# Graph layer with a mixture of experts on one core: the second norm and the router's scores inside the last edge group, edge steps numbered through all groups, token lists in bf16

## The reference

```
xn = layernorm(x)
x = x + segment_sum(edge_weight[:, None] * xn[dst], src, 6250) + mix(xn)     # gnn term: see below
t = layernorm(x)
logits = t @ router_w.T                     # 8 experts
probs = softmax(logits); rw, re = top_k(probs, 2); rw = rw / sum(rw)
moe = t
for e in range(8):
    moe = moe + combine[:, e:e+1] * (gelu(t @ w1[e] + b1[e]) @ w2[e] + b2[e])
out = x + moe
```

## Time and profile before

| | |
|---|---|
| Time, median of 3 runs (lowest, highest) | 2516.29 us (2516.20, 2521.94) |
| The profiled execution | 2519.71 us, its span 2518.0 us |
| Mean granted clock of PE | 0.941 of full speed |
| Busy: PE | 2169.8 us, 86% |
| Busy: POOL | 1509.9 us, 60% |
| Busy: DVE | 1468.8 us, 58% |
| Busy: ACT | 1141.0 us, 45% |
| DMA, mean over the span | 107 GB/s |

### The profile page before, as it was taken

The page is one execution under the profiler, slowest core; times in us unless marked ns, Lnnn a source line. Parts: engine busy times, 40 slices in busy tenths (PEclk is TensorE's granted clock), DMA queues, the critical chain, the costliest instruction groups (busy, mean ns, idle before and its releaser), DMA issues. The chain is left out here.

```text
span 2518.0 us, 38803 instructions
## 1 busy us (share of the span) xinstructions
PE 2169.8 (86%) x11962; PEld 1810.5 (72%) x11963; DVE 1468.8 (58%) x2640; ACT 1141.0 (45%) x3408; POOL 1509.9 (60%) x1295
## 2 busy tenths in 40 slices
PE   5798689988998899889988998899999856887884
PEld 3486578877887788678877887788777755665553
DVE  7994577667766775677577757775333566000112
ACT  4420245555555455545554555455565310333332
POOL 1002677677767766777676767776666421555553
PEclk9998899999999899999999999999999757899997
DMA  7424622232222222222232222222333311555666
GB/s 236 164 63 156 215 72 83 83 90 70 84 85 88 71 81 82 88 74 82 81 90 73 81 82 84 80 82 81 90 88 88 110 52 44 174 177 171 193 197 211
DMA packets 156966, 270.51 MB, mean 107 GB/s; under 512 B 27733, under 2 KB 104548, under 8 KB 156808
## 3 DMA queue, kind: packets, MB, share of 16 engines
q0 software_dynamic: 59584, 161.78, 21.4%
q1 hardware_dynamic: 62220, 72.81, 9.2%
q10 hardware_dynamic: 35004, 33.93, 4.4%
HBM read 223.61 MB, written 45.77 MB: 107 GB/s over the span
## 5 line engine op out<-in xcount | busy, mean ns | idle before, releaser
L1124 POOL DMA_INDIRECT edge_G<-xn_scratch,edge_row_i x1029 | 1226.1, 1192 | 452.1 <-issue 279.2
L1185 ACT ACTIVATE edge_weighted<-edge_hots,bins_scale 128x128 f32<-128x128 bf16 x2401 | 738.4, 391 | 66.4 <-DVE edge_row_hots L1213 66.4
L1153 PE MATMUL edge_op<-edge_win,edge_A 128*128 128x256 f32 x2744 | 671.5, 388 | 43.9 <-issue 33.9
L1153 PEld LDWEIGHTS edge_op<-edge_win,edge_A 128*128 128x128 f32 x2744 | 526.5, 194 | 144.3 <-issue 55.1
L1149 PE MATMUL edge_op<-edge_G,edge_weighted 128*128 128x256 f32 x2058 | 517.0, 388 | 67.7 <-DMA edge_G<-xn_scratch,edge_row_i 48.3
L1176 ACT COPY edge_A<-edge_ap 128x512 f32<-128x512 f32 x343 | 201.1, 586 | 767.5 <-PE edge_ap L1140 632.8
L1208 DVE TENSOR_TENSOR edge_hots<-bins_iota128b,bins_recb 128x1024 bf16<-128x1024 bf16 x343 | 236.8, 690 | 419.9 <-PE edge_ap L1140 328.4
L1149 PEld LDWEIGHTS edge_op<-edge_G,edge_weighted 128*128 128x128 f32 x2058 | 370.9, 194 | 113.4 <-issue 51.8
L1140 PE MATMUL edge_ap<-edge_weighted,edge_row_hots 128*128 128x128 f32 x2744 | 370.4, 278 | 25.6 <-DMA edge_win<-xn_scratch 13.3
L1140 PEld LDWEIGHTS edge_ap<-edge_weighted,edge_row_hots 128*128 128x128 f32 x2744 | 341.4, 193 | 60.0 <-issue 19.2
L1213 DVE TENSOR_TENSOR edge_row_hots<-all_iota,bins_recd 128x512 f32<-128x512 f32 x343 | 235.0, 685 | 0.0
(11 more groups left out here) (286 smaller groups left out, 1906.5 us busy)
## 6 DMA issues: line engine op xcount, KB each, us to landing
exp_w1x<-in_w ACTq DMA_DIRECT2D x105, 256.0 KB
edge_G<-xn_scratch,edge_row_i POOLq DMA_INDIRECT x1029
exp_ys<-ys_scratch SPq DMA_DIRECT2D x12, 1024.0 KB
ln_xin<-in_x SPq DMA_DIRECT2D x12, 512.0 KB, 5.5
xn_scratch<-ln_xnb ACTq DMA_DIRECT2D x12, 512.0 KB, 5.9
xnT_scratch<-ln_xT SPq DMA_DIRECT2D x12, 512.0 KB, 7.0
mix_xg<-xn_scratch SPq DMA_DIRECT2D x12, 512.0 KB, 3.9
mix_ek<-xnT_scratch SPq DMA_DIRECT2D x12, 512.0 KB, 4.8
```

The costliest lines, as they stand in the source:

```text
L1124: pool.indirect_dma_start(out=G[:, row_buffer(b), i, :], out_offset=None, in_=xn_dram, in_offset=bass.IndirectOffsetOnAxis(ap=row_i[:, b * ...
L1153: last = nc.tensor.matmul(op[j][:, :], A[:, j, i, :], win[:, q % 2 * DN + i, :], start=False, stop=i == DN - 1)
L1185: last = nc.scalar.activation(weighted[:, buf, i, :], hots[:, b % 2, i // 2, :, i % 2], ACT.Copy, scale=scale[:, b, i:i + 1])
```

## The change

1. Edge steps are numbered t = q * NB + b through all groups. The gathered rows have five buffers (t % 5), POOL may issue when step t - 5 has ended, and `row_i` has two halves, so that its copy waits for no rows. The weighted one-hots have two buffers in place of three.
2. `pe_share` is called between the window product (L1140) and the gathered product (L1149) of a step, in place of after L1153.
3. `norm2_block` is gone. In group 6, the last, step b also does for earlier tiles: DVE `measure(b - 2)` and `normalise(b - 4)`, with the addition of hn to h that POOL had; ACT `root(b - 3)` and `turn_out(b - 6)`; PE, between L1140 and L1149, `turn(b - 5)` and `score(b - 7)`; SP stores hn tile by tile. The scratch lies in the space of SL. After step 48 the remaining tiles follow, then the scores are copied to `logits`, then the flag is worked out. The stage for the flag's other case gets a norm of its own.
4. The loads of b2, w2 and b1 start with the routing stage.
5. The list stage works in bf16 on pairs of tiles. A token's number is split in two: the tile's number and an entry's own part, so `value` has 210 columns in place of 105, and a token is 256 times the first plus the second.

```diff
 class Bins:
-        self.diag = st.sb("diag", [NCH, NCH])
-        self.ones_f = st.sb("ones_f", [NCH, P])
+        self.spare = SL[:, :].bitcast(F32)
+        self.ones_f = self.raw[0:NCH, 0, :, :].rearrange("p v b -> p (v b)")[:, 0:P]
+        self.diag = self.raw[0:NCH, 0, :, :].rearrange("p v b -> p (v b)")[:, P:P + NCH]
...
-        self.bp = [st.ps(f"bp{j}", [P, self.NV * NB]) for j in range(2)]
+        self.bp_all = [st.ps(f"bp{j}", [P, D]) for j in range(2)]
+        self.bp = [b[:, 0:self.NV * NB] for b in self.bp_all]
...
 def edge_stage(...)
-        NE, BEFORE = bins.NE, 3
+        NE, AHEAD = bins.NE, 5
-        row_i = st.sb("row_i", [P, NB * GN], I32)
+        row_i = st.sb("row_i", [P, 2, NB * GN], I32)
-        weighted = st.sb("weighted", [P, 3, CB, P])
+        weighted = st.sb("weighted", [P, 2, CB, P])
-        G = st.sb("G", [P, 4, GN, D])
+        G = st.sb("G", [P, AHEAD, GN, D])
+        tp = bins.bp_all
+        scores = bins.base[1][:, 0:NT * NEXP].rearrange("p (t e) -> p t e", e=NEXP)
...
             def _(sp):
+                sp.wait_ge(bins.half_binned, NQ * bins.HALVES)
+                sp.dma_start(rws, router_w).then_inc(rw_in, 16)
+                for t in range(NT):
+                    r = rows_of(t)
+                    sp.wait_ge(hn_done, t + 1)
+                    sp.dma_start(hn_dram[t * P:t * P + r, :], hnb[0:r, t % HB, :]).then_inc(hn_out[t % HB], 16)
...
             def _(pool):
                     pool.wait_ge(bins.rows_ready, q + 1)
-                    if q > 0:
-                        for j in range(4):
-                            pool.wait_ge(gathered[j], q * USES[j] * 16 * GN)
-                        if q * NB + b >= 3:
-                            pool.wait_ge(stepped, q * NB + b - 2)
+                        t = q * NB + b
+                        if t >= AHEAD:
+                            pool.wait_ge(stepped, t - AHEAD + 1)
                         for i in range(GN):
                             pool.indirect_dma_start(
-                                out=G[:, row_buffer(b), i, :], out_offset=None, in_=xn_dram,
+                                out=G[:, t % AHEAD, i, :], out_offset=None, in_=xn_dram,
...
             def _(pe):
+                def turn(t):
+                    r = rows_of(t)
+                    pe.wait_ge(hn_done, t + 1)
+                    if t >= 2:
+                        pe.wait_ge(evacuated, t - 1)
+                    for k in range(KC):
+                        last = transpose(nc, tp[t % 2][:, k * P:k * P + r], hnb[0:r, t % HB, k * P:(k + 1) * P], ident, r)
+                    last.then_inc(turned, 1)
+                def score(t):
+                    r = rows_of(t)
+                    pe.wait_ge(evacuated, t + 1)
+                    for k in range(KC):
+                        last = nc.tensor.matmul(scores[0:r, t, :], hnT[:, t % 2, k, 0:r], rwT[:, k, :],
+                                                start=k == 0, stop=k == KC - 1)
+                    last.then_inc(scored, 1)
+                def route(b):
...
+                    if 0 <= b - 5 < NT:
+                        turn(b - 5)
+                    if 0 <= b - 7 < NT:
+                        score(b - 7)
                 def products(q, b):
...
                     last.then_inc(a_done, 1)
+                    if q + 1 < NQ:
+                        bins.pe_share(pe, q + 1, b)
+                    else:
+                        route(b)
                     if t >= 2:
-                        pe.wait_ge(summed, t - (0 if b == 0 else 1))
-                    pe.wait_ge(gathered[rb], (q * USES[rb] + (1 if rb == 3 else b // 3 + 1)) * 16 * GN)
+                        pe.wait_ge(summed, t - 1)
+                    pe.wait_ge(gathered[rb], (t // AHEAD + 1) * 16 * GN)
...
                         products(q, b)
-                        if q + 1 < NQ:
-                            bins.pe_share(pe, q + 1, b)
+                for b in range(NB, NB + 8):
+                    route(b)
...
             def _(act):
+                def root(t):
+                    act.wait_ge(var_done, 2 * t + 2)
+                    if t >= HB:
+                        act.wait_ge(rstd_done, t - HB + 1)
+                    nc.scalar.activation(std[0:r, t % HB:t % HB + 1], mv[0:r, t % HB, 1:2], ACT.Sqrt, ...)
+                def turn_out(t):
+                    act.wait_ge(turned, t + 1)
+                    if t >= 2:
+                        act.wait_ge(scored, t - 1)
+                    nc.scalar.copy(hnT[:, t % 2, :, 0:r], tp[t % 2]...)
...
             def _(dve):
+                def measure(t):
+                    nc.vector.bn_stats(stats[0:r, t % 2, :], h[0:r, t, :]).then_inc(var_done, 1)
+                    nc.vector.bn_aggr(mv[0:r, t % HB, :], stats[0:r, t % 2, :]).then_inc(var_done, 1)
+                def normalise(t):
+                    dve.wait_ge(std_done, t + 1)
+                    nc.vector.reciprocal(rstd[...], std[...]).then_inc(rstd_done, 1)
+                    if t >= HB:
+                        dve.wait_ge(turned, t - HB + 1)
+                        dve.wait_ge(hn_out[t % HB], 16 * (t // HB))
+                    nc.vector.tensor_scalar(hnb[...], h[0:r, t, :], mv[...], rstd[...], ALU.subtract, ALU.mult).then_inc(hn_done, 1)
+                    nc.vector.tensor_tensor(h[0:r, t, :], h[0:r, t, :], hnb[0:r, t % HB, :], ALU.add).then_inc(h_done, 1)
...
                             bins.dve_share(dve, q + 1, b)
+                        else:
+                            route(b)
...
+                nc.vector.tensor_copy(logits[:, 0:NT - 1, :], scores[:, 0:NT - 1, :])
+                nc.vector.tensor_copy(logits[0:TAIL, NT - 1, :], scores[0:TAIL, NT - 1, :])
...
-def norm2_block(...)
...
 def route_block(...)
             def _(sp):
+                sp.dma_start(b2e[:, :], b2).then_inc(wx_in, 16)
+                sp.dma_start(w2s[:, :, :, :], w2.rearrange("e (c p) f -> p e c f", p=P)).then_inc(wx_in, 16)
+                    for k in range(KC):
+                        sp.dma_start(b1T[:, k, :], b1[:, k * P:(k + 1) * P].rearrange("e p -> p e")).then_inc(wx_in, 16)
                 sp.wait_ge(act_c, EXPED + 3)
...
 def list_block(...)
+    T2 = (NT + 1) // 2
-    PIECES = [(k, a, b) for k in range(2) for a, b in ((0, NT // 2), (NT // 2, NT))]
+    PIECES = [(k, a, b) for k in range(2) for a, b in ((0, T2 // 2), (T2 // 2, T2))]
-        value = st.sb("value", [P, 2, NT, NXT])
-        rows = st.sb("rows", [P, 2, NT, P])
-        listed = st.ps("listed", [P, NXT])
+        at = st.sb("at", [P, 2, T2, NXT, 2], BF16)
+        value = st.sb("value", [P, 2, T2, 2, NXT, 2], BF16)
+        rows = st.sb("rows", [P, 2, T2, P, 2], BF16)
+        listed = st.ps("listed", [P, 2 * NXT])
...
-                        last = nc.tensor.matmul(listed[:, :], rows[:r, k, t, :], value[:r, k, t, :],
+                        last = nc.tensor.matmul(listed[:, :], rows[:r, k, t // 2, :, t % 2],
+                                                value[:r, k, t // 2, :, :, t % 2].rearrange("p v c -> p (v c)"),
...
+                    link(v.tensor_tensor(at[:, k, a:b, :, :], over_pairs(line, a, b), of_pairs(in_tile[:, k, :], a, b, NXT),
+                                         ALU.is_equal))
+                    v.tensor_tensor(value[:, k, a:b, 0, :, :], at[:, k, a:b, :, :], of_pairs(tile_b, a, b, NXT), ALU.mult)
+                    v.tensor_scalar(value[:, k, a:b, 1, :, :], at[:, k, a:b, :, :], own[:, k:k + 1], None, ALU.mult)
+                    v.tensor_tensor(rows[:, k, a:b, :, :], over_pairs(slot, a, b), of_pairs(in_row[:, k, :], a, b, P),
+                                    ALU.is_equal).then_inc(made, 1)
                 dve.wait_ge(summed, 1)
-                link(v.tensor_copy(found[:, :], listed[:, :]))
+                link(v.tensor_copy(low[:, :], listed[:, NXT:2 * NXT]))
+                link(v.scalar_tensor_tensor(found[:, :], listed[:, 0:NXT], float(2 * P), low[:, :], ALU.mult, ALU.add))
```

More of the change, by code:

```diff
@@ L1069, in edge_stage @@
         weighted_done = bins.weighted_done
-        gathered = [st.sem(f"gathered{j}") for j in range(4)]
+        gathered = [st.sem(f"gathered{j}") for j in range(AHEAD)]
         a_done = st.sem("a_done")
@@ L1341, in _, with root @@
                         tile(t)
+                    def root(t, r):
+                        wait_then_pass(pool, normed, t * NORM + 3, passed["pool"])
+                        nc.gpsimd.tensor_tensor(rstd[0:r, :], var[0:r, :], half[0:r, :], ALU.pow).then_inc(rooted, 1)
+                    with pool.Fori(0, NT - 1) as t:
+                        root(t, P)
+                    root(NT - 1, TAIL)
             @block.tensor
@@ L1353, in _, with score @@
                         nc.tensor.matmul(merged[:, :], same[:, :], msg[:, :], start=True, stop=True).then_inc(merge_done, 1)
+                    def score(t, r):
+                        wait_then_pass(pe, normed, t * NORM + 4, passed["pe"])
```

(28 more changed lines are left out.)

426 lines of the change are left out of this document (181 added, 245 removed).

## The result

The changed kernel took 2413.05 us (median of four runs, 2407.20 to 2419.75) against 2516.24 for the kernel before: a ratio of 0.958 (95% interval 0.956 to 0.960). Its profiled execution took 2407.2 us, with a span of 2404.2 against 2518.0: 113.8 us less, where the sum of the prediction was 115.9.

A forecast was written before the change was run, and what follows sets the result against it. It saw PE's waits for gathered rows in the edge stage, a half-clock norm stage and a DVE-bound list stage. Terms -71.3 + 8 + 5.8 - 44 + 0.9 - 15.3 = -115.9 from 2519.7 gave 2401 us at the median's level, range 2378 to 2422.

The forecast's parts named there:

- The norm stage and its tail: Norm stage removed, -71.3 us; the last tiles' norm and scores after the last product, +5.8 (4 to 8).
- The last group: Norm work inside group 6: 4.70 us a step in place of 4.53, +8 us (bounds +3.5 and +33).
- 0.1 of lateness: Last group: of 0.60 us a step of lateness, 0.1 stays, as new PE work partly lies over it.
- Groups 0 to 5: Edge groups before the last: gather waits and half-clock time cut, -44 us; near 237 us each.
- Five row buffers ... -44: Edge groups 0 to 5: three quarters of 48.3 us gather waits gone, 36, plus 8 of half-clock time.
- pe_share ... Cost 0: Binning matmuls moved before the gathered product: they cover late copies, SL is ready early enough, cost 0.
- 15 us more cover: Edge stage: POOL may run four steps ahead in place of two, 15 us more cover against 2 to 3 us delays.
- Rival 1: Groups 0 to 5: gather waits end but DVE or late semaphores stand next, gain 0 there; 2445 us; chance 0.16.
- Routing and list: Weight loads moved to routing, +0.9 us (0 to 2); list stage in bf16 pairs, -15.3 (-8 to -18).
- Rival 4: Groups 0 to 5: moved binning matmuls make PE wait for SL in 168 steps; 2535 us at 0.8 each; chance 0.01.
- Rival 2: Last group not covered: POOL's issues grow beside DVE's passes or lateness stays, 5.2 a step, +25; 2426 us; chance 0.15.
- Rival 3: Groups 0 to 5: gather waits, lateness and half clock all vanish, -95 us; 2350 us; chance 0.13.

The follow-up runs named there:

- both steps taken back: Changed kernel with three row buffers and the binning matmuls behind the window matmuls; ratio 0.972 on the chip where the kernel before took 2397 us.
- the two small steps: Changed kernel with POOL's select before the split of b2 and list pieces of 13 and 12 pairs; 2420.7 us against 2415.9 beside it.

## Why the prediction was right, and where it was not

**The norm stage and its tail.** -71.0 and +6.5 against -71.3 and +5.8. Right by its own terms: the last hn came 4.0 us after the last finish, as forecast.

**The last group.** +6.1 against +8. PE's new work there, by the rows of the window from 1714 to 1939.8 (a few records lie outside it or are missing), is 21.9 us for 172 records of scores (L1174) and 17.5 for 91 of transposes (L704), and PE stood only 3.6 us in front of the window product:

```profile
L1221 PE MATMUL edge_op<-edge_win,edge_A 128*128 128x256 f32 x392 | 92.9, 380 | 3.6 <-issue 3.6
...
L1245 ACT COPY edge_A<-edge_ap 128x512 f32<-128x512 f32 x49 | 28.7, 586 | 77.2 <-PE edge_ap L1204 54.7 <-issue 14.9 <-remote 7.6
...
L1174 PE MATMUL bins_base<-all_rwT,bins_SL 128*128 128x8 f32 x172 | 21.9, 236 | 0.0
...
L704 PE MATMUL bins_bp<-all_ident,bins_SL 128*128 128x128 f32 x91 | 17.5, 273 | 0.0
```

The step became 4.6 us, the floor that I had worked out, so 0.1 of lateness was too much. But the reason given for it, that the work in front of the gathered product lies over late copies, was wrong: behind the window matmuls it costs the same on both kinds of chip. The late copies themselves went, from 30 us to 4 to 6. What fits, and is not shown, is that POOL's three issues, 3.8 us with their gaps, filled a step of 4.5 us with 3.9 of work nearly whole, and leave more room in one whose own work is 4.6; this was not tried by itself. With three buffers it was 5 as well, so the buffers aren't it.

**Groups 0 to 5.** -41.7 against -44, the right sum for a wrong reason. The step that failed is "Five row buffers ... -44" together with "pe_share ... Cost 0". The gather waits did end, wholly and not by three quarters. But in the one set on a common chip five buffers raised the late copies from 48 to 101 us and the wait for them from 24.8 to 65.5, and the groups took 7.9 us more with five than with three (1426.5 against 1418.6). That is within the 15 us by which these groups differ between traces with the same edge stage (1432.2, 1440.3, 1447.1). More than half of the gain came from the place of the binning matmuls, which I had costed at nothing: 22 and 23 us on the two kinds of chip.

What is left of the 42 us, some 20, is not shown. It would have to stand with what none of these runs took back, above all the numbering through the groups: at the starts of groups 1 to 5 PE had stood 1.1 to 3.4 us each, 14 in all, for rows (3.39 in the earlier trace rows), and now stands there no more. On the quick chip less can be left for it. With both steps taken back the kernel still gained 63.5 us there (2396.5 to 2333.0). The stages behind the groups would make 78.3 of them by the common chip's numbers. Against them stands the last group, 220.2 us now, and before hardly less than 49 undisturbed steps of 3.93, 192.6 us. So by this estimate some 13 us at most are left. The sum's "15 us more cover" was wrong too: two more steps of 5.0 us are 10.

Rival 1, waits that move, was half true: on the common chips they moved to late semaphores, and another gain paid for it. This is one such copy in the trace of the changed kernel:

```profile
859.44 1.05 PE L1204 MATMUL edge_ap<-edge_weighted,edge_row_hots 128*128 128x128 f32 x8
...
861.33 1.46 PE L1217 MATMUL edge_op<-edge_G,edge_weighted 128*128 128x256 f32 x6
...
863.22 0.96 POOL L1154 DMA_INDIRECT edge_G<-xn_scratch,edge_row_i  x1 [0.30 <-issue]
864.48 0.96 POOL L1154 DMA_INDIRECT edge_G<-xn_scratch,edge_row_i  x1 [0.30 <-issue]
865.75 0.96 POOL L1154 DMA_INDIRECT edge_G<-xn_scratch,edge_row_i  x1 [0.30 <-issue]
866.44 0.59 ACT L1245 COPY edge_A<-edge_ap 128x512 f32<-128x512 f32 x1 [7.94 <-remote]
...
867.08 2.72 PE L1221 MATMUL edge_op<-edge_win,edge_A 128*128 128x256 f32 x8 [4.29 <-ACT edge_A L1245]
```

The product at 859.44 ended by 860.5. ACT, idle for 7.94 us, copied at 866.44, some 6 us late; PE had done its other work by 862.8 and stood 4.29 us. POOL issued one gather after the other all the while. The prediction had called the same thing in the last group lateness without a cause; the cause lies with POOL's indirect DMAs, their issue or the queue that they go through, shown by the two kernels in which they were gone or fewer.

Why the place of binning pays is argued, not shown: in front, it gives DVE's addition and the rows a microsecond more in 28 steps a group. PE's wait in front of the gathered product fell with it from 44.7 to 25.7 us on the quick chip, which is most of the 22 us (this is its row with the binning behind):

```profile
L1215 PE MATMUL edge_op<-edge_G,edge_weighted 128*128 128x256 f32 x2058 | 511.6, 385 | 44.7 <-DVE all_xn L1324 23.4
```

On the common chip it fell from 22.9 to 17.3 only. There PE's idle time in groups 0 to 5 is 13 us less in all (95 to 82), and the other 10 us are matmuls that took less time, at a granted clock of 0.984 against 0.981.

**Routing and list.** +0.9 and -14.7 against +0.9 and -15.3. In the list the tensor_scalar was 0.87 for twelve pairs as taken (0.8), but 1.63 for thirteen, at the upper bound (1.47 for twelve is 1.59 for thirteen) and not at the value. The last matmuls took 4.1 us where 4.0 was forecast.

**Rival 4** (PE waits for SL): PE stood 4.2 us in all in front of binning matmuls in the edge stage, in five cases over 0.3 us. **Rival 2** didn't happen: the last group took 225.3 us, not 244, and POOL's issues in it had a mean of 1.02 us, as before, so DVE's new passes did not lengthen them. **Rival 3** was far off on a common chip, but the kernels without lateness show its floor: 222.8 us a group.

## What to carry to other kernels

Before a wait for data is bought off with more buffers, look at what else the producer's engine does when it may run free: here, on the common chips, signals of another engine were seen late while POOL's indirect DMAs went out in long rows, and the wait moved one instruction on. Work without dependants, put between a product and the wait behind it, paid by itself. A sum that comes out right says nothing of its terms: only taking one term back at a time, on one chip, did.

## What the runs showed of the hardware

- On the common chips ACT saw the end of PE's product up to 10.6 us late (in the run of the two small steps), and DVE with it (both at 866.44 in the copy shown), mostly while POOL issued indirect DMAs one behind the other; with one gather a step, or with the same bytes fetched by SP, not once in 343 steps. Whether the issuing or its queue holds them up stays open, and so does why five buffers doubled it in the one pair of traces that differ in nothing else up to the last group.
- The quick chip had none of this in four traces, with up to 147 issues in a row, and its expert stage took 347 to 356 us against 389 to 398. The same kernels gave 2397 us there and 2501 to 2523 elsewhere. Five buffers were worth 31 us there and nothing on another. Why that chip differs stays open.
- A bf16 tensor_scalar of 2520 elements in 12 pairs of tiles took 0.87 us, and one of 2730 in 13 took 1.63, in whichever order they stood.
